# Attention over 16 heads of width 8: from masked 106-row matmuls to one 32-row group per head

## The chip, the cores and the metric

The kernel runs on one NeuronCore of a Trainium2 chip. The metric is the device time of one launch in microseconds (us), the median of three runs. The program was also run once under the hardware profiler; all rows shown here come from that one execution.

## The reference

Four blocks follow one another on x of shape (4, 1024, 128), float32: attention with an ALiBi bias, a mixture of nine experts, a linear attention with decay, and the experts again. Only the first is touched by the change:

```python
q, k, v = proj(Wq, bq), proj(Wk, bk), proj(Wv, bv)        # (4, 1024, 16 heads, 8) from layernorm(x)
scores = jnp.einsum('bqhd,bkhd->bhqk', q, k) / sqrt(8)
scores = scores + bias[None, :, None, :]                  # -(slope of the head * key position)
attn = jax.nn.softmax(scores, axis=-1)
out = jnp.einsum('bhqk,bkhd->bqhd', attn, v).reshape(B, L, D)
x = x + out @ Wo.T + bo
```

## The kernel before

`build_program` calls `attention_phase`, then `expert_phase`, `decay_phase` and `expert_phase`. Everything below is in `attention_phase` (L160 to L710).

The work is cut into 16 units: four sequences b times four groups g of four heads. Within a unit the softmax needs the largest score of each query ahead of the exponentials, so every score is computed twice. `score_unit` (L317, matmul L325) makes scores with queries on partitions, 128 queries by 512 keys, and VectorE takes their maximum (`take_max`, L571): 64 such tiles for a unit, eight query tiles by four heads by two halves of the keys. `tscore` (L329, matmul L335) makes them again transposed, 128 keys by 512 queries, with the negated maximum as two more rows of the contraction, and ScalarE takes the exponential (`exponential`, L499). `values` (L349, matmul L361) multiplies the exponentials of four heads with the padded values `Vp`, float32, each head into its own 32 partitions of bankO.

Precision is kept by splitting queries and keys in a high and a low part (float32r), stacked three times 32 rows: high-high, low-high, high-low. All four heads of the group share these 96 rows of Q. K exists once per head, with the other heads' rows zeroed by a mask (L690, on GpSimd). Rows 96 and 97 carry the bias, rows 98 to 105 the maxima of four heads in two parts. So every score matmul contracts over 98 or 106 rows.

A unit is 16 blocks, k = 0 to 15: two halves of the queries (qh) by eight key tiles (kt). Each engine has its order written out. In a block TensorE issues

```python
tscore(k, 0) score(0) tscore(k, 1) score(1) values(k - 1) tscore(k, 2) score(2) tscore(k, 3) score(3) [extra]
```

where the scores are those of a later unit (three blocks ahead, `AHEAD`), and the extra is one item of `MISC` (L230): a projection for the unit after next (`project`, L305), the transposes of the result (`transpose_u`, L369, and `transpose_on`, L377), the output projection (L384), or `aux` (L313), which brings the maxima from `M2` back through TensorE into rows of Q. All extras share one bank, bankM. bankT and bankS are rings of three banks each; `values(k - 1)` waits until the four exponentials of block k - 1 are done (L359). ScalarE copies the sums out of bankO after each half (`take_u`, L504), and the first `values` of the next half waits for it. Most units run in a hardware loop over b.

Ahead of the blocks stand the layer norm, as a phase with a barrier at its end, and the 64 score tiles of unit 0, which VectorE's maxima pace. In the last unit no scores of a later unit are left, so TensorE issues only tscore and values.

Of the kernel before, what the change touches and what calls it, by code (L numbers as in the profile page):

```python
# [9 lines left out]
ds = bass.ds  # L10
# [149 lines left out]
def attention_phase(nc, X, XT, ident, ident_in, c, w, load, scratch):  # L160
# [7 lines left out]

    AUX = 3 * GE
    NROW_S = AUX + 2
    NROW_T = NROW_S + 2 * HG
    ROTATE = 3

    def last_user(u, units):


        return u - ROTATE if u >= ROTATE else max(v for v in range(units) if v % ROTATE == u) - units

    with ExitStack() as ctx:
# [3 lines left out]
        Wq3 = sb("Wq3", [D, G, AUX]); Wk3 = sb("Wk3", [D, G, AUX])  # L185
        bq3 = sb("bq3", [AUX, G]); bk3 = sb("bk3", [AUX, G]); bq3s = sb("bq3s", [AUX, G])
        WvT = sb("WvT", [D, D]); WoT = sb("WoT", [D, D])
        bvb = sb("bvb", [P, D]); bob = sb("bob", [P, D])
        masks = sb("masks", [AUX, HG])
        V = sb("V", [P, TILES, D])  # L190
        Vp = sb("Vp", [P, TB, H, VW])
        Q = [sb(f"Q{g}", [P, L], F32R) for g in range(G)]
        K = [sb(f"K{g}", [P, HG, L], F32R) for g in range(G)]
        Tq = sb("Tq", [AUX, L]); Tk = sb("Tk", [AUX, L]); Kc = sb("Kc", [AUX, L])
        E = sb("E", [P, 2, HG, BANK])
        hmax = sb("hmax", [P, 2, TB * HG, QH])
        nmax = sb("nmax", [P, TB, HG])
        M2 = sb("M2", [P, TB, VW])
        U = sb("U", [P, L])
        rden = sb("rden", [P, TH * HG])  # L200
        On = sb("On", [P, TB, D])
        ones = U
        OnT = sb("OnT", [P, L])

        (w_loaded, const_loaded, bias_set, zero_done, x_biased) = sem(
            "w_loaded", "const_loaded", "bias_set", "zero_done", "x_biased")
        (proj_ready, proj_taken, q_high, k_high, k_low, k_copies, q_done, k_done) = sem(
            "proj_ready", "proj_taken", "q_high", "k_high", "k_low", "k_copies", "q_done", "k_done")
        (score_ready, max_taken, max_joined, max_high, aux_in, aux_ready, aux_taken) = sem(
            "score_ready", "max_taken", "max_joined", "max_high", "aux_in", "aux_ready", "aux_taken")  # L210
        (tscore_ready, exp_done, pv_done, u_taken) = sem("tscore_ready", "exp_done", "pv_done", "u_taken")
        (ut_ready, rden_done, on_done, ont_ready, ont_taken, y_ready, y_added) = sem(
            "ut_ready", "rden_done", "on_done", "ont_ready", "ont_taken", "y_ready", "y_added")
        (v_ready, v_taken, vp_done) = sem("v_ready", "v_taken", "vp_done")

        S_UNITS = TB * HG * QH
        T_UNITS = QH * TB * HG
        BLOCKS = QH * TB
        PER_BLOCK = S_UNITS // BLOCKS
        AHEAD = 3  # L220

        def score_units(k, now, later):


            m = PER_BLOCK * (k + AHEAD)
            ahead, m = 1 + m // S_UNITS, m % S_UNITS
            return [(ahead, m + i) for i in range(PER_BLOCK)] if (now, later)[ahead - 1] else []


        MISC = {1: ("K", 0), 2: ("K", 1), 3: ("Q", 0), 4: ("Q", 1), 5: ("T", 0), 6: ("T", 1),  # L230
                8: ("G", 0), 9: ("G", 1), 11: ("Y", 0), 12: ("Y", 1), 14: ("A", 0), 15: ("A", 1)}

        def misc(k, s, project, score, after):

            kind, h = MISC.get(k, (None, 0))
            ok = {"K": project, "Q": project, "A": score, "T": after, "G": after and s == 0,
                  "Y": after and s == 0}.get(kind, False)
            return (kind, h) if ok else None

        weights = ((Wq3[:], w["Wq3"]), (Wk3[:], w["Wk3"]), (bq3[:], w["bq3"]), (bk3[:], w["bk3"]),  # L240
                   (WvT[:], w["WvT"]), (WoT[:], w["WoT"]), (masks[:], c["masks"]),
                   (bvb[:], w["bv"].partition_broadcast(P)), (bob[:], w["bo"].partition_broadcast(P)))

        zeros = sb("zeros", [P, BANK])
        zeros_set, cleared = sem("zeros_set", "cleared")

        def load_all(sp, loaded):
            load(sp, loaded)
            for dst, src in weights:
                sp.dma_start(dst, src).then_inc(w_loaded, 16)  # L250

            sp.wait_ge(zeros_set, 1)
            for place in scratch.values():
                sp.dma_start(place.rearrange("(p n m) d -> p n (m d)", p=P, m=BANK // D),
                             zeros[:].unsqueeze(1).broadcast_to([P, SLOT_TILES * D // BANK, BANK]))\
                    .then_inc(cleared, 16)
            sp.wait_ge(w_loaded, 16 * len(weights))

        def constants(block):
            @block.gpsimd  # L260
            def _(pool):
                for g in range(G):
                    pool.dma_start(K[g][AUX:NROW_T, :, :].rearrange("p h k -> p (h k)"), c["key_aux"][g])\
                        .then_inc(const_loaded, 16)
                count = [0]

                def alone(ins):

                    count[0] += 1
                    ins.then_inc(zero_done, 1)  # L270
                    pool.wait_ge(zero_done, count[0])
# [21 lines left out]
        with nc.Block() as block:  # L293
            @block.sync
            def _(sp):
                sp.wait_ge(cleared, 16 * len(scratch))
# [1490 lines left out]
```

## Time and profile before

| | |
|---|---|
| median of three runs | 1989.09 us (1988.19 to 1992.72) |
| span of the profiled execution | 2086.8 us |
| TensorE, VectorE, ScalarE, GpSimd busy | 1651.1, 1093.8, 902.5, 571.8 us |
| first tscore of unit 0 | 100.2 us from the start |
| last values of unit 15 | 1016.8 us from the start |

The profiled execution's own time is its span, 2086.8 us, the time from its first to its last instruction; no other time of it is given. It is 4.9% above the median of the unprofiled runs. Times in the rows are counted from the start of that span. A matmul record ends later than the next can start, since matmuls are pipelined: the distance between starts tells the pace.

### The profile page before, as it was taken

The numbers are of one execution on the slowest core, as the hardware profiler recorded it, in microseconds if no ns is written. First come the engines' busy times: TensorE is split into PE (matmuls) and PEld (weight loads), VectorE is DVE, ScalarE is ACT, GpSimd is POOL, SyncE is SP. The second block draws the span as 40 slices with busy tenths as digits, with TensorE's granted clock in tenths as the row PEclk, the third lists the DMA queues.
The fourth block names the chain that finished last, engine by engine and source line by source line (L and its number), as shares of the span: only waits on it lengthen the run. The fifth ranks groups of instructions, "written<-read, shape, count | busy, mean of one in ns | idle before, by whom it ended". The sixth has DMA issues, their size and how long they took to land. (4 is left out here: it accounts for less than half of the span.)

```text
span 2086.8 us, 32437 instructions
## 1 busy us (share of the span) xinstructions
PE 1651.1 (79%) x8928; PEld 953.1 (46%) x8929; DVE 1093.8 (52%) x2392; ACT 902.5 (43%) x1760; POOL 571.8 (27%) x548
## 2 busy tenths in 40 slices
PE   4899999999999999999632698902899972289890
PEld 2544544545454544554331576701444442167670
DVE  5877777777777777774232122224455553222222
ACT  2266666666666666667510243404222210034340
POOL 3422222112222222110054105453212205410635
PEclk7899999999999999999856899955999985589995
DMA  9000000000000000000121112110000001111222
GB/s 268 1 1 1 1 1 1 3 1 1 1 1 2 1 1 1 1 1 1 42 90 54 45 55 70 56 50 11 1 1 0 0 3 39 55 49 50 74 72 66
DMA packets 69399, 61.23 MB, mean 29 GB/s; under 512 B 8296, under 2 KB 59624, under 8 KB 68840
## 3 DMA queue, kind: packets, MB, share of 16 engines
q1 hardware_dynamic: 39824, 31.66, 4.9%
q0 software_dynamic: 8320, 17.45, 3.0%
q10 hardware_dynamic: 21120, 10.49, 1.8%
q8 instruction: 64, 1.05, 0.2%
q14 instruction: 71, 0.58, 0.1%
HBM read 28.12 MB, written 31.46 MB: 29 GB/s over the span
## 5 line engine op out<-in xcount | busy, mean ns | idle before, releaser
L571 DVE TENSOR_REDUCE attn_hmax<-attn_bankS 128x1 f32<-128x512 f32 x1024 | 644.9, 684 | 206.9 <-PE attn_bankS L325 203.3
L499 ACT ACTIVATE attn_E<-attn_bankT 128x512 f32<-128x512 f32 x1024 | 546.7, 598 | 272.1 <-PE attn_bankT L335 266.3
L335 PE MATMUL attn_bankT<-attn_Q,attn_K 106*128 106x512 f32 x1024 | 458.5, 454 | 5.3 <-ACT attn_E L499 3.1
L325 PE MATMUL attn_bankS<-attn_K,attn_Q 98*128 98x512 f32 x1024 | 418.8, 415 | 22.6 <-DVE attn_hmax L571 17.7
L335 PEld LDWEIGHTS attn_bankT<-attn_Q,attn_K 106*128 106x128 f32 x1024 | 192.3, 189 | 274.5 <-ACT attn_E L499 237.8
L1208 DVE TENSOR_TENSOR ffn_hidden<-ffn_bank,ffn_gated 128x352 f32<-128x352 f32 x160 | 83.9, 525 | 371.8 <-ACT ffn_gated L1167 296.6
L361 PE MATMUL attn_bankO<-attn_E,attn_Vp 128*32 128x512 f32 x2048 | 272.7, 604 | 6.5 <-ACT attn_U L504 5.4
L325 PEld LDWEIGHTS attn_bankS<-attn_K,attn_Q 98*128 98x128 f32 x1024 | 197.2, 193 | 96.8 <-DVE attn_hmax L571 50.5
L1101 PE MATMUL ffn_bank<-w,ffn_xT 128*128 x640 | 226.3, 478 | 7.2 <-issue 4.2
L684 POOL TENSOR_TENSOR attn_Kc<-attn_Tk,attn_Kc 32x1024 f32<-32x1024 f32 x15 | 35.6, 2373 | 667.9 <-DVE attn_Kc L563 667.9
L1016 POOL DMA_INDIRECT tokens<-ffn_XN,ffn_slots x128 | 124.0, 969 | 309.5 <-DVE ffn_slots L885 234.5
L1253 POOL DMA_INDIRECT ffn_pair<-results,ffn_slots x128 | 122.5, 957 | 311.7 <-DMA results<-ffn_y 211.3
L1167 ACT ACTIVATE ffn_gated<-ffn_bank 128x352 f32<-128x352 f32 x160 | 74.1, 463 | 240.6 <-PE ffn_bank L1101 176.2
L1592 DVE TENSOR_TENSOR decay_Am<-decay_bankA,decay_Dm 128x512 f32<-128x512 f32 x128 | 88.4, 690 | 117.5 <-PE decay_bankA L1446 117.3
L1123 PE MATMUL ffn_bankY<-w,ffn_hT 128*128 x960 | 140.7, 284 | 10.0 <-issue 9.9
L1446 PE MATMUL decay_bankA<-decay_qm,decay_km 128*128 128x512 f32 x256 | 140.6, 637 | 6.2 <-ACT decay_km L1543 6.2
L1101 PEld LDWEIGHTS ffn_bank<-w,ffn_xT 128*128 128x128 f32 x640 | 113.9, 198 | 47.9 <-issue 15.8
L1123 PEld LDWEIGHTS ffn_bankY<-w,ffn_hT 128*128 128x128 f32 x960 | 123.8, 197 | 18.2 <-issue 18.2
L1112 PE MATMUL ffn_bankH<-ident,ffn_hidden 128*128 128x128 f32 x480 | 82.2, 282 | 58.7 <-issue 51.7
L690 POOL TENSOR_TENSOR attn_K<-attn_Kc,attn_masks 96x1024 fp32r<-96x1024 f32 x60 | 118.0, 1995 | 2.3 <-POOL attn_Kc L684 2.1
L1112 PEld LDWEIGHTS ffn_bankH<-ident,ffn_hidden 128*128 128x128 f32 x480 | 62.2, 145 | 108.0 <-issue 84.2
L1173 ACT COPY ffn_hT<-ffn_bankH 128x384 f32<-128x384 f32 x160 | 76.0, 475 | 37.1 <-remote 21.3
(182 smaller groups left out, 1380.7 us busy)
## 6 DMA issues: line engine op xcount, KB each, us to landing
ffn_x<-tokens SPq DMA_DIRECT2D x40, 256.0 KB
results<-ffn_y ACTq DMA_DIRECT2D x40, 256.0 KB
tokens<-attn_zeros SPq DMA_DIRECT2D x1, 5120.0 KB, 16.8
results<-attn_zeros SPq DMA_DIRECT2D x1, 5120.0 KB, 28.8
X<-in_x SPq DMA_DIRECT2D x4, 512.0 KB, 16.0
tokens<-ffn_XN,ffn_slots POOLq DMA_INDIRECT x128
ffn_pair<-results,ffn_slots POOLq DMA_INDIRECT x128
out_dram<-X SPq DMA_DIRECT2D x4, 512.0 KB
```

The source lines that it names most:

```text
L325: nc.tensor.matmul(bankS[m % ROTATE][:], Q[g][0:NROW_S, qt * P:(qt + 1) * P], K[g][0:NROW_S, j, kh * BANK:(kh + 1) * BANK], start=True, st ...
L335: nc.tensor.matmul(bankT[u % ROTATE][:], K[g][0:NROW_T, j, kt * P:(kt + 1) * P], Q[g][0:NROW_T, qh * BANK:(qh + 1) * BANK], start=True, st ...
L361: last = nc.tensor.matmul(bankO[32 * j:32 * j + VW, :], Vp[:, kt, g * HG + j, :], E[:, k % 2, j, :], start=(kt == 0), stop=(kt == TB - 1))
L499: nc.scalar.activation(E[:, k % 2, j, :], bankT[(HG * k + j) % ROTATE][:], ACT.Exp)\
L571: nc.vector.reduce_max(hmax[:, g % 2, m // QH, m % QH:m % QH + 1], bankS[m % ROTATE][:], AX.X)\
L690: last = nc.gpsimd.tensor_tensor(K[g][0:AUX, j, :], Kc[:], masks[:, j:j + 1].broadcast_to([AUX, L]), ALU.mult)
L1016: pool.indirect_dma_start(tokens[:, :], bass.IndirectOffsetOnAxis(slots[:, t, k:k + 1], 0), XN[:, t, :], None).then_inc(scattered[h], 16)
L1101: last = nc.tensor.matmul(bank[:, 0:HID], xT[:, p, (k % TH) * P:(k % TH + 1) * P], W13[:, ds(e, 1), :], start=True, stop=True)
L1112: last = nc.tensor.transpose(bankH[:, t * P:(t + 1) * P], hidden[:, k % 2, t * P:(t + 1) * P], ident[:])
L1123: last = nc.tensor.matmul(bankY[k // TH][:, (k % TH) * P:(k % TH + 1) * P], hT[:, k % 2, t * P:(t + 1) * P], w2e[:, t * D:(t + 1) * D], st ...
L1253: pool.indirect_dma_start(pair[:, t % RING, k, :], None, results[:, :], bass.IndirectOffsetOnAxis(slots[:, t, k:k + 1], 0))\
L1446: nc.tensor.matmul(bankA[u % 2][:], km[:, p, j, b * P:(b + 1) * P], qm[:, p, :, b * P:(b + 1) * P], start=True, stop=True).then_inc(a_read ...
```

## The change

`attention_phase` is rewritten; the other phases stay.

- **Row groups.** Head j has rows 32j to 32j + 27 of Q and K: three times 8 rows for the parts, two for the bias, two for its maximum. K is no longer copied per head, and a score matmul contracts over 26 or 28 rows at partition 32j. The bias enters K through a small second matmul in the key projection. The split is four operations of 128x1024 on GpSimd per unit.
- **Maxima.** Two matmuls fill a pair of banks with 128 queries by 1024 keys; one reduce of 128x1024 takes the negated maximum. There are 512 such pairs. bankS is a ring of two pairs, and the transposes of the result and the output projection (`U`, `Y`) take slots in it.
- **T ring.** bankT has three banks, which also serve projections (`P`), transposes of the normalised output (`N`) and the prelude. bankM is gone.
- **Spreading the maxima.** After the 16 pairs of a half (4 query tiles by 4 heads), VectorE splits them in two parts, transposes in 32x32 squares (`turn_maxima`), and SyncE moves them into rows 26 and 27 of each group of Q by eight DMAs. The first exponent of the half waits for all eight.
- **Lead.** Maxima run 22 pairs (`LEAD`, eleven blocks) ahead of the exponents; the turn of half h comes after pair 16h + 19, two blocks ahead of the half's first block 8h.
- **Prelude and form.** The layer norm's work stands inside the same block, with no barrier behind it; all loops are unrolled. Padding of the values moves from VectorE to GpSimd, with two buffers.

```diff
+                def maximum(i, kh):
+                    h, m = divmod(i, ITEMS)
+                    n, qh = divmod(h, QH)
+                    qt, j = qh * TH + m // HG, m % HG
...
+                    rows = slice(32 * j, 32 * j + NROW_S)
+                    mm = nc.tensor.matmul(bank[:, kh * BANK:(kh + 1) * BANK], Q[n % G][rows, qt * P:(qt + 1) * P],
+                                          K[n % G][rows, kh * BANK:(kh + 1) * BANK], start=True, stop=True)
+                def exponent(kb, j, opens):
+                    h, kt = divmod(kb, KT)
+                    n, qh = divmod(h, QH)
+                    if opens and kt == 0:
+                        pe.wait_ge(max_in[h % 2], 16 * 8 * (h // 2 + 1))
+                    bank = slot(("E", kb, j))
+                    rows = slice(32 * j, 32 * j + NROW_T)
...
+        def t_extra(kb):
+
+            n, k = divmod(kb, QH * KT)
+            if k in (6, 8, 10, 12) and n + 2 < UNITS:
+                return ("P", n + 2, (k - 6) // 2)
+            if n % G == 0 and n and k in (7, 9):
+                return ("N", n // G - 1, (k - 7) // 2)
+            return None
+
+        def s_extra(kb):
+
+            n, k = divmod(kb, QH * KT)
+            if k == 3 and n:
+                return ("U", n - 1)
+            if n % G == 0 and n and k == 12:
+                return ("Y", n // G - 1)
+            return None
+
+        def order(kb):
+            return (0, 3, 1, 2) if kb % 2 == 0 else (2, 1, 3, 0)
...
+                for kb in range(BLOCKS):
+                    i = 2 * kb + LEAD
+                    js = order(kb)
+                    exponent(kb, js[0], True)
+                    if i < MAXIMA:
+                        maximum(i, 0)
+                    exponent(kb, js[1], False)
+                    if i < MAXIMA:
+                        maximum(i, 1)
+                    if kb:
+                        values(kb - 1)
+                    exponent(kb, js[2], False)
+                    if i < MAXIMA:
+                        maximum(i + 1, 0)
+                    exponent(kb, js[3], False)
+                    if i < MAXIMA:
+                        maximum(i + 1, 1)
...
+                def spread_maxima(h):
+                    n, qh = divmod(h, QH)
+                    sp.wait_ge(max_turned, h + 1)
+                    for e in range(MAX_ROWS):
+                        rows = Q[n % G][MAX0 + e:P:32, qh * BANK:(qh + 1) * BANK].bitcast(F32)
+                        rows = rows.rearrange("j (t a r) -> j a t r", t=TH, a=4)
+                        for a in range(4):
+                            sp.dma_start(rows[:, a], MT[32 * a + HG * e:32 * a + HG * (e + 1), :, :])\
+                                .then_inc(max_in[h % 2], 16)
...
+                    nc.vector.tensor_reduce(nmax[:, h % 2, m // HG, m % HG:m % HG + 1], bank[:], AX.X, ALU.max,
+                                            negate=True).then_inc(s_taken, 1)
...
+                        if ITEMS <= i < MAXIMA + ITEMS and i % ITEMS == 3:
+                            turn_maxima(i // ITEMS - 1)
```

## Rows read from the trace of the kernel before

**Rows 1.** The page: span, TensorE's busy time, granted clock in 40 slices.
```profile
span 2086.8 us, 32437 instructions
PE 1651.1 (79%) x8928; PEld 953.1 (46%) x8929; DVE 1093.8 (52%) x2392; ACT 902.5 (43%) x1760; POOL 571.8 (27%) x548
...
PEclk7899999999999999999856899955999985589995
```

**Rows 2.** Busy time by stretch: length, busy (count) by engine, clock, DMA share.
```profile
400.00:700.00 300.00, 290.97 (x1491) 150.09 (x1489) 225.97 (x375) 197.67 (x371) 63.22 (x30) 1.00 0.01 1
```

**Rows 3.** Groups: line, engine, out<-in, count | busy us, mean ns | idle before, releaser.
```profile
L335 PE MATMUL attn_bankT<-attn_Q,attn_K 106*128 106x512 f32 x1024 | 458.5, 454 | 5.3 <-ACT attn_E L499 3.1 <-ACT attn_Q L492 2.2
...
L361 PE MATMUL attn_bankO<-attn_E,attn_Vp 128*32 128x512 f32 x2048 | 272.7, 604 | 6.5 <-ACT attn_U L504 5.4 <-ACT attn_E L499 0.9
L571 DVE TENSOR_REDUCE attn_hmax<-attn_bankS 128x1 f32<-128x512 f32 x1024 | 644.9, 684 | 206.9 <-PE attn_bankS L325 203.3 <-DVE attn_On L594 2.8
...
L594 DVE TENSOR_TENSOR attn_On<-attn_bankM,attn_rden 128x128 f32<-128x128 f32 x32 | 9.3, 292 | 1.1
L499 ACT ACTIVATE attn_E<-attn_bankT 128x512 f32<-128x512 f32 x1024 | 546.7, 598 | 272.1 <-PE attn_bankT L335 266.3 <-issue 5.0
L695 POOL TENSOR_TENSOR attn_Q<-attn_Tq,attn_Q 32x1024 fp32r<-32x1024 f32 x15 | 35.6, 2374 | 2.8 <-POOL attn_K L690 2.0 <-DVE attn_Q L567 0.7
```

**Rows 4.** Timeline of TensorE, middle of unit 6: start us, us, instruction, count.
```profile
502.06 0.40 PE L335 MATMUL attn_bankT<-attn_Q,attn_K 106*128 106x512 f32 x1
502.29 0.39 PE L325 MATMUL attn_bankS<-attn_K,attn_Q 98*128 98x512 f32 x1
502.61 1.06 PE L361 MATMUL attn_bankO<-attn_E,attn_Vp 128*32 128x512 f32 x8
503.61 0.50 PE L335 MATMUL attn_bankT<-attn_Q,attn_K 106*128 106x512 f32 x1
```

**Rows 5.** Timeline of TensorE, then ScalarE, in the last unit.
```profile
998.09 1.07 PE L361 MATMUL attn_bankO<-attn_E,attn_Vp 128*32 128x512 f32 x8 [0.48 <-ACT attn_U L504]
...
1003.43 1.06 PE L361 MATMUL attn_bankO<-attn_E,attn_Vp 128*32 128x512 f32 x8
1004.43 0.96 PE L335 MATMUL attn_bankT<-attn_Q,attn_K 106*128 106x512 f32 x3
1005.62 0.50 PE L335 MATMUL attn_bankT<-attn_Q,attn_K 106*128 106x512 f32 x1 [0.23 <-ACT attn_E L499]
1006.10 1.07 PE L361 MATMUL attn_bankO<-attn_E,attn_Vp 128*32 128x512 f32 x8
...
1004.97 2.07 ACT L499 ACTIVATE attn_E<-attn_bankT 128x512 f32<-128x512 f32 x4 [0.60 <-PE attn_bankT L335]
```

**Rows 6.** SyncE's queue, two issues; a DMA's size and time to landing.
```profile
18.90 0.43 SPq L250 DMA_DIRECT2D attn_masks<-const_masks  x1
19.37 0.43 SPq L250 DMA_DIRECT2D attn_bvb<-weight_bv  x1
...
decay_WqT<-weight_b_WqT SPq DMA_DIRECT2D x1, 64.0 KB, 1.8
```

**Rows 7.** Timeline of TensorE: extras in the blocks.
```profile
516.54 1.02 PE L305 MATMUL attn_bankM<-XT,attn_Wk 128*96 x2
...
988.47 0.60 PE L369 MATMUL attn_bankM<-ident,attn_U 128*128 128x128 f32 x4
```

**Rows 8.** Timeline of TensorE: the same operation before and after idling.
```profile
89.73 1.03 PE L313 MATMUL attn_bankM<-ident,attn_M 128*32 128x128 f32 x8 [1.57 <-DVE attn_M L584]
91.44 1.92 PE L313 MATMUL attn_bankM<-ident,attn_M 128*32 128x128 f32 x8 [0.68 <-ACT attn_Q L492]
```

**Rows 9.** Timelines: VectorE's first maxima, TensorE's first tscore and last values.
```profile
45.15 4.87 DVE L571 TENSOR_REDUCE attn_hmax<-attn_bankS 128x1 f32<-128x512 f32 x8 [0.95 <-PE attn_bankS L325]
...
100.24 0.63 PE L335 MATMUL attn_bankT<-attn_Q,attn_K 106*128 106x512 f32 x1
...
1016.80 1.06 PE L361 MATMUL attn_bankO<-attn_E,attn_Vp 128*32 128x512 f32 x8 [0.94 <-ACT attn_E L499]
```

More of the change, by code:

```diff
@@ L214, in attention_phase @@
[L214 to L231, printed above, removed]
@@ new lines, in pair, with turn_tokens @@
+                def pair(item):
+                    i = s_at[item]
+                    if i >= S_PAIRS:
+                        pe.wait_ge(s_taken, i - S_PAIRS + 1)
+                    return bankS[i % S_PAIRS]
+                def turn_tokens(q):
+                    pe.wait_ge(normed, q + 1)
+                    bank = slot(("X", q))
+                    for t in range(TH):
+                        last = nc.tensor.transpose(bank[:, t * P:(t + 1) * P],
+                                                   xn[:, q % XN_SLOTS, t * P:(t + 1) * P], ident[:])
+                    last.then_inc(t_ready, 1)
@@ L473, in _, with turn_values @@
-                for h in range(2):
-                    pe.wait_ge(*free_at[0])
-                    out_project(B - 1, h)
-                    free_at[0] = (y_added, 2 * (B - 1) + h + 1)
+                def turn_values(n):
+                    pe.wait_ge(u_taken, QH * (n + 1))
+                    bank = pair(("U", n))
+                    for t in range(Q_TILES):
+                        last = nc.tensor.transpose(bank[:, t * P:(t + 1) * P], U[:, t * P:(t + 1) * P], ident[:])
+                    last.then_inc(s_ready, 1)
@@ new lines, in turn_outputs, with out_project @@
+                def turn_outputs(b, h):
+                    pe.wait_ge(s_taken, s_at["U", G * (b + 1) - 1] + 1)
+                    bank = slot(("N", b, h))
+                    for t in range(TH):
+                        last = nc.tensor.transpose(bank[:, t * P:(t + 1) * P], On[:, h * TH + t, :], ident[:])
+                    last.then_inc(t_ready, 1)
+                def out_project(b):
+                    pe.wait_ge(t_taken, t_at["N", b, 1] + 1)
+                    bank = pair(("Y", b))
+                    for t in range(Q_TILES):
+                        last = nc.tensor.matmul(bank[:, t * D:(t + 1) * D], OnT[:, t * P:(t + 1) * P], WoT[:],
+                                                start=True, stop=True)
+                    last.then_inc(s_ready, 1)
@@ new lines, in _ @@
+                for kb in range(BLOCKS):
+                    for j in order(kb):
+                        exponent(kb, j)
+                    if kb and kb % KT == 0:
+                        take_sums(kb // KT - 1)
+                    extra = t_extra(kb)
+                    if extra and extra[0] == "P":
+                        take_projection(extra[1], extra[2])
+                    elif extra:
+                        take_outputs(extra[1], extra[2])
+                take_sums(HALVES_A - 1)
```

787 lines of the change are left out of this document (362 added, 425 removed).

## The prediction, made before the changed kernel ran

> **What bounds the kernel now.** I read the page first: TensorE is busy 79% of a span of 2086.8 us, and its clock is full through the attention [rows 1]. The table of stretches then says who sets the pace there: from 400 to 700 us TensorE is busy 291 of 300 us, VectorE 226, ScalarE 198 [rows 2]. The groups say with what: 1024 transposed and 1024 direct score matmuls and the value matmuls; VectorE's and ScalarE's idle time ends at TensorE's scores, while TensorE hardly waits for anybody [rows 3]. The timeline gives prices. Two neighbouring score matmuls start 0.23 us apart, whether they contract over 98 or 106 rows; the four value products occupy 1.00 us from start to the next score, and the matmul ahead of them costs 0.32 instead of 0.23 [rows 4]. A plain block is then 8 x 0.235 + 1.19 = 3.07 us of TensorE, and with the extras 256 blocks fill the stretch from 100.24 to 1016.80 us, 916.6 us [rows 9].
>
> The last unit shows what stands behind TensorE. There the four direct scores of a block are gone, and still a block takes 1006.10 - 1003.43 = 2.67 us, although TensorE needs only 4 x 0.235 + 1.19 = 2.13 [rows 5]. It is a loop through two engines: values start; 1.00 us later the third exponent matmul of the block; 0.54 us after that ScalarE begins; two exponentials, 0.49 + 0.60 us (four take 2.07), end at 2.63; then the next values may start, 0.04 later. The order of issue makes this loop, since exponents 2 and 3 of block k stand behind values(k - 1) and ahead of values(k). The new order keeps it.
>
> **The change, part by part.** *Row groups.* The arithmetic per matmul falls, but a matmul's 512 columns cost what they did. The gain can only come from neighbours in different row groups running at once. No matmul of that kind is in the trace; the nearest rows are the value products, whose four column groups together take 1.00 us for eight records of 0.60 [rows 3, 4]. The order 0,2,3,2 | values | 1,3,2,3 lets two or three overlap. Bounds for the eight: serial 1.88 us, two at a time 0.94. TensorE has 2.67 - 1.19 = 1.48 us for them before it binds, 0.185 us each. I take the lower end, as the column groups do the like, and so a block of 2.67 us, set by the loop: 256 x 2.67 = 683.5 us. The Trainium skill (TensorE: Matmul & The Clock Gate, Part 3) states a measured 3.07 times for four row tiles of 512 columns, by which the eight would take 0.61 us; no run here shows it yet, and the block would be 2.67 all the same.
>
> *Two banks at once.* VectorE spaces 128x512 reduces by (4.87 - 0.68)/7 = 0.60 us [rows 9]. One over 1024 columns lies between 0.60 and 1.20; I take 1.20, as the columns dominate: 2.40 us a block, under the loop, hence worth nothing in the blocks. The ring of two pairs holds: a pair refilled behind values has 2.67 us to be read.
>
> *Sums.* Each half keeps its wait for the copy out of bankO, 0.48 us [rows 5]: 32 x 0.48 = 15.4.
>
> *Maxima spread by DMA.* What leaves is 32 calls of aux, 1.03 us of TensorE each [rows 8], which are part of the 916.6. What comes is a chain with a wait at its end, and everything later in TensorE's queue (direct scores, values) stands behind that wait, and with it VectorE and ScalarE. Count from the start of the values in block 8h - 2. The last matmul of pair 16h + 19 starts at 1.00 + 0.10 + 0.21 = 1.31, its record ends at 1.71, the reduce runs 1.81 to 3.01, the 32x32 transpose (a 128x128 operation of VectorE took 0.29 [rows 3]) ends at 3.30. SyncE issues eight DMAs, 0.47 us apart whatever their size: 3.3. The last lands after 1.8, if as fast as the quickest load [rows 6]: 8.4, and the first exponent of block 8h can start at 8.5, its values at 9.0. Without the wait they would start at 2 x 2.67 = 5.3. So each half but the first stalls 3.7 us: 31 x 3.7 = 114.7. Bounds: issue 0.43 apart and landing at 1.3 gives 2.9; landing at 2.8 gives 4.7. The Trainium skill (DMA: Bandwidth & Descriptors, Anatomy of one DMA) gives about 2.0 us of fixed cost per DMA; with it the stalls would be 6 us more in all.
>
> *Clock.* TensorE idles about 4.3 us in each stall. After an idle time of only 1.57 us the same eight records went from 1.03 to 1.92 us [rows 8], full to half clock. A block at half clock costs 0.85 more for values and about 0.35 more for the exponent ahead of ScalarE, 1.2; part of the low stretch lies in the stall itself, so I take 0.8 a half, 24.8 in all. Bounds: nothing, and four blocks of 1.2.
>
> *Extras.* A projection (1.02 us [rows 7]) now takes a slot of the T ring: the second exponent of the next block waits for the exponential two places on, and values move from 2.67 to about 3.2. Of four in a unit the one at k = 6 falls into the stall: 14 x 3 x 0.6 = 25.2. U takes a pair: the next pair waits for VectorE until 3.1, values start at 3.6: 15 x 0.95 = 14.3. Y and N: 3 x 3.1 = 9.3. GpSimd's four operations at up to 2.4 us [rows 3] are 9.5 us per unit of 54, two units ahead: hidden; uncovered they would cost that once.
>
> Sum: 683.5 + 15.4 + 114.7 + 24.8 + 25.2 + 14.3 + 9.3 = 887.2, against 916.6: 29.4 less.
>
> *Prelude.* Eleven weight loads issue at 0.47 from about 16 us and are in at about 25; four projections at half clock end near 34; 18 more items of at most 1.02 us [rows 7] end near 52.5; 20 reduces of 1.20 and three small operations reach 77.3, the eight DMAs 82.6, against 100.24 [rows 9]: 17.6 less. The end (one copy, two transposes, one addition instead of a chain through one bank) saves some 1.5. Unrolled code costs nothing visible, as unit 0 was unrolled before too.
>
> In all 48.5 us less: 2087 to 2038 us for the profiled execution. That execution is 98 us above the median, and I can't say where; none of my terms rests on a rare delay, so I subtract the same from the median: 1989 - 49 = **1940 us**.
>
> **Rivals.** *(a) The groups don't overlap.* Then TensorE binds at 3.07 us and pays its extras on top, while the stall stays (the turn comes later with the slower block, 3.7): 16 x (49.1 + 7.4 + 6.0) = 1000, less 25 for the last two units that lack projections and scores, 975; with the clock 25: 83 more than 916.6, prelude and end 19 less: about 2053 us. For it: each matmul loads its own 128 columns of weights, and no row group runs beside another in this trace. Against: column groups do. It decides from about 0.22 us a matmul upwards; a block of 2.92 instead of 2.67 eats the 49 us.
>
> *(b) The maxima are in time.* If issue and landing took under 1.6 us together there is no stall and no fall of the clock: 887 - 115 - 25 = 747, about 1989 - 170 - 19 = 1800 us. Against: eight issues alone take 3.3 us. Between this and the forecast lies a half stall, 1870.
>
> *(c) The clock stays low after stalls*, three to four blocks each time: 31 x 4.2 = 130 instead of 25: about 2045 us. For it: the fall after 1.57 us. Against: through the attention it stayed full [rows 1], in the last unit too, where TensorE needs 2.13 of 2.67 us.
>
> *(d) The change does as its numbers suggest* and VectorE's 2.4 us set the block. Then 256 blocks are 69 us shorter, but the stall grows by 0.54 each: 1888 us. The Trainium skill (TensorEngine Tiling (Array Packing), PSUM Bottleneck) says that the copy out of PSUM may become the bound once tiles run side by side; the loop of the last unit, 2.67, speaks against it.
>
> **How the numbers follow.** Chances: forecast 0.56, (a) 0.15, (b) and the half stall 0.13, (c) 0.10, (d) 0.06. The forecast's own range is 1890 to 1990: stalls of 2.9 to 4.7 are -25 to +31, a block 0.1 longer 19, clock and prelude 20. The range for 8 in 10 is 1850 to 2035: it leaves out the full (b) and the upper parts of (a) and (c). A measurement of this kernel tells 0.2%, 4 us, from no change. Faster: 0.51 of the forecast's 0.56, (b), (d) and a small part of (c): 0.72. Within 0.2%: 0.04. Slower: (a), most of (c): 0.24.
>
> **What would show it.** Two score matmuls of different groups starting some ns apart, and eight in under 1.48 us; values 2.67 us apart in a plain block; VectorE busy about 85% between stalls; 32 times a wait of TensorE's for the DMAs into Q, ending about 5.2 us after the transpose; half clock for a few us behind it; first exponent near 83 us. The forecast is wrong if the issue of a DMA of 16 runs of 128 bytes is much cheaper than 0.47 us, if the groups run one by one, or if the clock doesn't come back.

## The result: 2332 us, a ratio of 1.172

The changed kernel takes 2332.45 us (median of four runs, 2327.18 to 2335.98) against 1989.26: 1.172 times the kernel before, 95% interval 1.1692 to 1.1748. The forecast was 1940, at most 2035. Sign and size are both wrong.

The page of the changed kernel; the groups give busy us and mean ns, then the idle time before them:

```profile
span 2328.9 us, 28004 instructions
PE 1902.9 (82%) x8704; PEld 828.2 (36%) x8705; DVE 1026.3 (44%) x1850; ACT 891.5 (38%) x1728; POOL 497.2 (21%) x519
...
PEclk9555555555555555555555555999758999669995
...
L585 DVE TENSOR_REDUCE attn_nmax<-attn_bankS 128x1 f32<-128x1024 f32 x512 | 618.0, 1223 | 615.4 <-PE attn_bankS L365 615.4
L504 ACT ACTIVATE attn_E<-attn_bankT 128x512 f32<-128x512 f32 x1024 | 550.0, 597 | 615.2 <-PE attn_bankT L377 613.9
L377 PE MATMUL attn_bankT<-attn_Q,attn_K 28*128 28x512 f32 x1024 | 464.9, 756 | 108.9 <-DMA attn_Q<-attn_MT 62.9
L365 PE MATMUL attn_bankS<-attn_K,attn_Q 26*128 26x512 f32 x1024 | 549.6, 713 | 4.1 <-DVE attn_nmax L585 3.6
...
L681 POOL TENSOR_SCALAR attn_highk<-attn_Tk,attn_lowk 128x1024 fp32r<-128x1024 f32 x16 | 17.9, 1121 | 662.7 <-ACT attn_Tk L492 605.1
```

Its table of stretches, with columns as in [rows 2], for the same 300 us:

```profile
400.00:700.00 300.00, 278.60 (x1042) 84.77 (x1042) 148.80 (x148) 140.83 (x261) 30.11 (x17) 0.51 0.00 1
```

The clock row has a 5 where [rows 1] has a 9: for nearly all the time from 52 to 1370 us TensorE was granted half clock, 1.2 instead of 2.4 GHz. In the stretch the clock is 0.51 instead of 1.00, and TensorE is busy 279 of 300 us with 1042 instead of 1491 records. VectorE and ScalarE wait for it, over 600 us each. A matmul record of 713 to 756 ns is the same instruction that takes about 490 at full clock, as TensorE's timeline around one of the few rises shows (L338 is a projection, L413 the output projection, L391 the values):

```profile
465.14 2.08 PE L338 MATMUL attn_bankT<-XT,attn_Wq 128*128 128x512 f32 x2
467.01 2.71 PE L413 MATMUL attn_bankS<-attn_WoT,attn_OnT 128*128 128x128 f32 x16
469.65 0.50 PE L377 MATMUL attn_bankT<-attn_Q,attn_K 28*128 28x512 f32 x1
469.65 0.49 PE L365 MATMUL attn_bankS<-attn_K,attn_Q 26*128 26x512 f32 x1
469.65 0.50 PE L377 MATMUL attn_bankT<-attn_Q,attn_K 28*128 28x512 f32 x1
469.99 0.39 PE L365 MATMUL attn_bankS<-attn_K,attn_Q 26*128 26x512 f32 x1
470.31 1.07 PE L391 MATMUL attn_bankO<-attn_E,attn_Vp 128*32 128x512 f32 x8
471.30 0.49 PE L377 MATMUL attn_bankT<-attn_Q,attn_K 28*128 28x512 f32 x1
...
472.54 0.50 PE L377 MATMUL attn_bankT<-attn_Q,attn_K 28*128 28x512 f32 x1
...
473.03 1.06 PE L391 MATMUL attn_bankO<-attn_E,attn_Vp 128*32 128x512 f32 x8
...
475.27 0.67 PE L377 MATMUL attn_bankT<-attn_Q,attn_K 28*128 28x512 f32 x1 [0.21 <-ACT attn_E L504]
475.87 1.94 PE L391 MATMUL attn_bankO<-attn_E,attn_Vp 128*32 128x512 f32 x8
...
481.89 0.79 PE L377 MATMUL attn_bankT<-attn_Q,attn_K 28*128 28x512 f32 x1 [2.94 <-DMA attn_Q<-attn_MT]
```

Three things are to be seen. Matmuls of different row groups start together, three at 469.65, and the four with the switch to values take 0.66 us. A plain block at full clock is 473.03 - 470.31 = 2.72 us. And the clock falls at 475.27, when the score records go from 0.50 to 0.67 and the values from 1.06 to 1.94, six us after it rose and **before** TensorE waits for the DMA at 481.89. It rose right behind a projection and among sixteen matmuls of the output projection, all over 128 rows; there are three such rises, at 470, 795 and 1121 us. The other two ended with a wait of 4.4 us for the DMAs, about 10 us after the rise.

The clock had been lost long before the first such wait. In the prelude, where each pair of maxima waits for VectorE, it falls at 52 us; the first exponent waits for its DMAs at 79 (TensorE's timeline):

```profile
50.70 0.73 PE L365 MATMUL attn_bankS<-attn_K,attn_Q 26*128 26x512 f32 x2 [0.40 <-DVE attn_nmax L585]
51.84 0.95 PE L365 MATMUL attn_bankS<-attn_K,attn_Q 26*128 26x512 f32 x2 [0.41 <-DVE attn_nmax L585]
52.97 2.35 PE L365 MATMUL attn_bankS<-attn_K,attn_Q 26*128 26x512 f32 x4 [0.18 <-DVE attn_nmax L585]
```

From there it stayed at half until the output projection at 468 us. The kernel before also lost it in its prelude, at 91 us [rows 8], but its own score matmuls over 98 and 106 rows, one behind another, brought it back 14 us later:

```profile
104.08 0.63 PE L325 MATMUL attn_bankS<-attn_K,attn_Q 98*128 98x512 f32 x1
...
104.83 0.40 PE L325 MATMUL attn_bankS<-attn_K,attn_Q 98*128 98x512 f32 x1
```

A block at half clock on TensorE's timeline, then ScalarE's four exponentials of a block at full and at half clock:

```profile
582.83 1.94 PE L391 MATMUL attn_bankO<-attn_E,attn_Vp 128*32 128x512 f32 x8
584.69 0.79 PE L377 MATMUL attn_bankT<-attn_Q,attn_K 28*128 28x512 f32 x1
...
586.23 0.79 PE L377 MATMUL attn_bankT<-attn_Q,attn_K 28*128 28x512 f32 x1 [0.31 <-ACT attn_E L504]
...
586.96 1.94 PE L391 MATMUL attn_bankO<-attn_E,attn_Vp 128*32 128x512 f32 x8
```
```profile
471.89 2.07 ACT L504 ACTIVATE attn_E<-attn_bankT 128x512 f32<-128x512 f32 x4 [0.56 <-PE attn_bankT L377]
...
585.58 2.13 ACT L504 ACTIVATE attn_E<-attn_bankT 128x512 f32<-128x512 f32 x4 [1.93 <-PE attn_bankT L377]
```

The block takes 586.96 - 582.83 = 4.13 us. The loop: values start; after 1.86 us the exponent; after 0.89 ScalarE begins; after 0.65 (one exponential and the hand-over) the block's fourth exponent matmul, which waited 0.31 us for that T bank; 0.73 later the next values. At full clock the same steps are 0.99, 0.59, 0.65 and 0.49, in sum 2.72.

The stall at a half's start, on SyncE's queue and TensorE:

```profile
595.67 4.53 SPq L302 DMA_DIRECT2D attn_Q<-attn_MT  x8
```
```profile
601.30 0.79 PE L377 MATMUL attn_bankT<-attn_Q,attn_K 28*128 28x512 f32 x1 [0.54 <-DMA attn_Q<-attn_MT]
```

First exponent and last values of the attention, against 100.24 and 1016.80 in [rows 9]:

```profile
79.32 0.79 PE L377 MATMUL attn_bankT<-attn_Q,attn_K 28*128 28x512 f32 x1 [4.87 <-DMA attn_Q<-attn_MT]
...
1358.14 1.93 PE L391 MATMUL attn_bankO<-attn_E,attn_Vp 128*32 128x512 f32 x8 [1.23 <-ACT attn_E L504]
```

The attention ends 341 us later, which is the 343 of the medians. Counting the 255 distances between the values of neighbouring blocks, and calling a block full when its first value record took under 0.8 us: 8 full, of median 2.73, and 247 half, of median 4.13. I use this count ("full blocks") for every kernel below.

One caution for reading the ratios. The kernel before ran at 1989 us in some sets of runs (the results, e5 to e8 and e13 to e16) and at 2089 to 2093 in others (e1 to e4 and e9 to e12), so each ratio is to the kernel before in the same set. Ratios and their intervals are of the runs within 1.5% of a kernel's quickest, and medians are of all its runs. Where two sets are compared I use the time of the last values, which does not move (1016.8 and 1019.0 us in the kernel before at 2086.8 and 1988.3). Full blocks and last values are those of the profiled execution, which in e1, e7, e8 and e13 was the slowest of the runs or within 1 us of it.

### The profile page after: what moved, and what is told of

It reads as the page before. It is cut to its first block and busy times, and to the rows that moved or that the text cites. A ratio compares the mean times of both kernels' runs of the same rounds, so it can differ in the third digit from the quotient of the medians.

```text
span 2328.9 us, 28004 instructions
## 1 busy us (share of the span) xinstructions
PE 1902.9 (82%) x8704; PEld 828.2 (36%) x8705; DVE 1026.3 (44%) x1850; ACT 891.5 (38%) x1728; POOL 497.2 (21%) x519
## 5 line engine op out<-in xcount | busy, mean ns | idle before, releaser
L585 DVE TENSOR_REDUCE attn_nmax<-attn_bankS 128x1 f32<-128x1024 f32 x512 | 618.0, 1223 | 615.4 <-PE attn_bankS L365 615.4
L377 PE MATMUL attn_bankT<-attn_Q,attn_K 28*128 28x512 f32 x1024 | 464.9, 756 | 108.9 <-DMA attn_Q<-attn_MT 62.9
L365 PE MATMUL attn_bankS<-attn_K,attn_Q 26*128 26x512 f32 x1024 | 549.6, 713 | 4.1 <-DVE attn_nmax L585 3.6
L391 PE MATMUL attn_bankO<-attn_E,attn_Vp 128*32 128x512 f32 x2048 | 488.5, 1047 | 5.1 <-ACT attn_U L511 3.5
L377 PEld LDWEIGHTS attn_bankT<-attn_Q,attn_K 28*128 28x128 f32 x1024 | 176.8, 286 | 697.4 <-issue 379.9
L365 PEld LDWEIGHTS attn_bankS<-attn_K,attn_Q 26*128 26x128 f32 x1024 | 225.0, 295 | 22.2 <-DVE attn_nmax L585 19.3
L1098 PE MATMUL ffn_bank<-w,ffn_xT 128*128 x640 | 221.6, 470 | 6.0 <-ACT ffn_xT L1158 3.2
L681 POOL TENSOR_SCALAR attn_highk<-attn_Tk,attn_lowk 128x1024 fp32r<-128x1024 f32 x16 | 17.9, 1121 | 662.7 <-ACT attn_Tk L492 605.1
L391 PEld LDWEIGHTS attn_bankO<-attn_E,attn_Vp 128*32 128x32 f32 x2048 | 51.6, 139 | 138.8 <-ACT attn_E L504 59.3
```

The lines of the kernel that those rows point to most:

```text
L365: mm = nc.tensor.matmul(bank[:, kh * BANK:(kh + 1) * BANK], Q[n % G][rows, qt * P:(qt + 1) * P], K[n % G][rows, kh * BANK:(kh + 1) * BANK] ...
L377: nc.tensor.matmul(bank[:], K[n % G][rows, kt * P:(kt + 1) * P], Q[n % G][rows, qh * BANK:(qh + 1) * BANK], start=True, stop=True)\
L391: last = nc.tensor.matmul(bankO[32 * j:32 * j + VW, :], Vp[:, b % 2, kt, g * HG + j, :], E[:, kb % E_BLOCKS, j, :], start=(kt == 0), stop= ...
L585: nc.vector.tensor_reduce(nmax[:, h % 2, m // HG, m % HG:m % HG + 1], bank[:], AX.X, ALU.max, negate=True).then_inc(s_taken, 1)
L1098: last = nc.tensor.matmul(bank[:, 0:HID], xT[:, p, (k % TH) * P:(k % TH + 1) * P], W13[:, ds(e, 1), :], start=True, stop=True)
```

## The experiments

All leave the computation as it is; added matmuls write a bank that the next exponent overwrites. The theories have the letters of the expectations: **A**, the stream of matmuls over 26 and 28 of 128 rows doesn't hold the clock up, stall or no stall; **B**, the idle time of the stall for the DMAs brings it down and keeps it there; **C**, what counts is how much of the time some matmul runs, whatever its rows.

**e5 and e6: both kernels again, unchanged.**

> The changed kernel again, beside the kernel before on the chip of this call, since the runs of the kernel before lie at 1989 us in one call and at 2089 us in another. If only the kernel before differs between chips, this stays at about 2332 us and the ratio is 1.116; if both differ alike, it is near 2440 us and the ratio 1.17.

> The kernel before, unchanged, with a profile of its own, as a measure of what differs between two executions of one program: ratio 1.00. Its clock stays full from the first blocks to the last values, and the attention blocks fill 916 us as in the first profile; if the chips differ, it is in the stages behind them.

Measured: 2331.0 us, 1.1715 [1.1697, 1.1732], 8 full blocks; and 1989.64 us, 1.0001 [0.9982, 1.002]. The low clock repeats on another occasion.

**e1 and e7: the maxima earlier.** `AHEAD` counts blocks; the lead is 16 + 2 x `AHEAD` pairs. Six and five in place of three move the turn of the maxima from two blocks ahead of their use to five and four. The second line is a wait of VectorE's for its own earlier work.

```diff
-    AHEAD = 3
+    AHEAD = 6        (e7: 5)
...
+                    if n:
+                        dve.wait_ge(s_taken, s_at["U", n - 1] + 1)
```

> The lead of the maxima grows from three blocks to six, so that the DMAs into Q have landed before the half begins. Theory A (the clock falls because a score matmul fills 26 or 28 of 128 rows of the array): the waits for the DMAs vanish (2 to 3 us in each of 31 halves at half clock), the granted clock stays at 0.5 through the blocks, a plain block stays at 4.13 us, and the time is 2240 to 2280 us. Theory B (the idle time of the stall brings the clock down and keeps it there): with the stall gone the clock is full, a block is 2.7 us and the time below 1850 us.

> A lead of five blocks instead of three. The lead of six had a side effect: it moved the maxima's row groups onto those of the exponents beside them, so the overlap was partly lost; with five the groups stay apart and the DMAs still have time (two blocks more, 5.4 us at full clock, against the stall of 3.7 us). Theory A: half clock for most of the time, plain blocks of 4.13 us there, full clock for some tens of us behind each output projection; 2230 to 2270 us, within 1.5% of the lead of six. Theory B (idle time alone): mostly full clock, below 1900 us.

Measured: e1 2259.28 us, 1.0776 [1.072, 1.0832], 93 full blocks, last values at 1205.5. e7 2215.64 us over four runs from 2120.14 to 2263.72, without an interval, near 1.11; 15 full blocks in its profile (the slowest of the four), last values at 1290.6. No wait for a DMA stands in either; the stall is gone, and still most blocks are at half clock, so B alone is not it. Theory A had e7 about right (2230 to 2270 us). That e1 lies in its range (2240 to 2280) is luck: in that set the kernel before was 100 us slower than at the time of the forecast, and by the ratio the forecast was 1.13 to 1.15. TensorE's timeline of e1 at one fall:

```profile
586.38 1.06 PE L391 MATMUL attn_bankO<-attn_E,attn_Vp 128*32 128x512 f32 x8
...
588.62 0.50 PE L377 MATMUL attn_bankT<-attn_Q,attn_K 28*128 28x512 f32 x1
...
589.64 1.93 PE L391 MATMUL attn_bankO<-attn_E,attn_Vp 128*32 128x512 f32 x8 [0.53 <-ACT attn_U L511]
```

Here 0.53 us of idling, the wait for the copy out of bankO, was followed by half clock until 745 us; the kernel before has the like of it, 0.48 us in [rows 5], and stays full. In e1 itself nine such waits met full clock, and a fall stood right behind two of them and within a block of a third. Six also puts the maxima into the same row groups as the neighbouring exponents, so the later kernels use five.

**e2, e3, e4: more matmuls in each block.** Two at the start of every block, behind the wait for the maxima; over 128 rows in e2 and e4, over 28 in e3. e4 adds `AHEAD = 6`.

```diff
+                    if opens:
+                        for _ in range(2):
+                            nc.tensor.matmul(bank[:], K[n % G][:, kt * P:(kt + 1) * P],     (e3: [rows, ...])
+                                             Q[n % G][:, qh * BANK:(qh + 1) * BANK], start=True, stop=True)
```

> Two matmuls over all 128 rows (128x128 weights, 512 columns) are added at the start of each block; their result is overwritten by the first exponent matmul of the block, so the output doesn't change. The stall stays. Theory A: the array is filled enough, the clock is full, the two matmuls fit into the slack of the 2.67 us loop, and the time falls to 1900 to 1990 us although TensorE does more. Theory B: the stall is as before, the clock stays at half, and two more matmuls at 0.43 us make every block about 0.9 us longer: some 2550 us.

> The control of the run with two filling matmuls: the same two matmuls per block, but over the 28 rows of the head that follows. Theory A: as many matmuls and columns, but few rows, so the clock stays at half and each block is 0.85 to 0.9 us longer: 2500 to 2560 us. Theory C (what counts is how much of the time some matmul streams, whatever its rows): the clock rises as in the run with full rows, and the time is near 1950 us.

> Both: two matmuls over 128 rows in each block and a lead of six blocks. Both theories give full clock and no stall; theory A gives the block of 2.7 to 2.8 us set by the loop values, exponent matmul, two exponentials, values: 1810 to 1860 us, faster than both kernels. If the clock is full but the block is not 2.7 us, the loop was misread.

Measured: e2 2577.7 us, 1.2288 [1.2216, 1.236], 65 full blocks; e3 2466.11 us, 1.1802 [1.1784, 1.182], 9; e4 2372.85 us (2371.78, 2373.92, 2376.53 and once 2168.59), 170. Theory A's numbers for e2 and e4 missed by over 400 us, because I had taken the clock to be up all the time once filled; for e2, B's 2550 was nearer. In e3 neither C's 1950 nor A's 2500 to 2560 came: the narrow pair costs a block nothing (4.13 us at half clock, as without it), since it runs beside its neighbours. The wide rows do raise the clock (65 and 170 full blocks against 9), and with the stall in place it comes down again, in e2 13 of 14 times after 14 to 23 us. A block at half clock with the two costs 5.31 us, 1.18 more than 4.13, so filling pays only where the clock then stays.

**e8 and e9: lead, fill, and fill in the prelude; wide against narrow.** `AHEAD = 5` with its wait; two matmuls at the start of each block, ahead of the wait for the maxima, four more in block 6 of each unit, and three behind each pair of the lead.

```diff
+                def wide(bank, n, count):
+                    for _ in range(count):
+                        nc.tensor.matmul(bank[:], K[n % G][:, 0:P], K[n % G][:, 0:BANK], start=True, stop=True)
...
+                    if opens:
+                        wide(bank, n, 2 + (4 if kb % 16 == 6 else 0))
...
+                    wide(slot(("E", 0, order(0)[0])), 0, 3)      (in the loop over the lead)
```

In e9 the rows are `32 * j:32 * j + 28`.

> A lead of five blocks; two matmuls over 128 rows ahead of every block (operands from K alone, result overwritten), four more ahead of one block of each unit, and three behind each of the 26 leading pairs, so that the clock is up when the blocks begin. Theory A: the clock stays up nearly throughout; a plain block costs 1.0 (values) + 3 x 0.66 us = 2.98 us and the whole is 50 to 80 us below the kernel before. If the clock falls again and again, the share of half clock decides: 2250 us at one half of the time. Theory B gives full clock as well, so this run measures what full clock is worth, not which theory holds.

> The run with two wide matmuls per block and the wide lead, lead of five blocks, with one change: each added matmul runs over the 28 rows of one head instead of 128. Same places, same number, same columns. Theory A (rows filled decide the clock): half clock through nearly all blocks, ratio to the kernel before 1.10 to 1.18. Theory C (time streamed decides, rows don't matter): full clock as in the wide version, ratio 0.95 to 0.98.

Measured: **e8 1955.4 us** (1934.49 to 1967.95), 0.9746 [0.9718, 0.9773], or 0.983 by the medians, 244 full blocks, last values at 995.2, ahead of the kernel before. A block at full clock has the forecast 2.98 us. e9 2128.4 us, 1.0175 [1.0153, 1.0198], 165 full blocks, last values 1057.3. The clock row and the 300 us of e8:

```profile
PEclk8999997599999999999965899965899995599995
```
```profile
400.00:700.00 300.00, 297.04 (x1695) 112.41 (x1694) 219.53 (x218) 206.37 (x378) 37.23 (x21) 0.99 0.01 2
```

VectorE is busy 220 us where the changed kernel has 149: with the clock back the same code goes half as fast again. Both kernels do the same work with the same count of columns; only rows differ. In the prelude the narrow ones lose the clock (e9, then e8, TensorE's timeline; a lone L365 goes from 0.50 to 0.79 us):

```profile
56.73 0.50 PE L365 MATMUL attn_bankS<-attn_K,attn_Q 26*128 26x512 f32 x1
...
57.86 0.79 PE L365 MATMUL attn_bankS<-attn_K,attn_Q 26*128 26x512 f32 x1
```
```profile
57.73 0.73 PE L365 MATMUL attn_bankS<-attn_K,attn_Q 26*128 26x512 f32 x2
58.39 0.97 PE L372 MATMUL attn_bankT<-attn_K 128*128 128x512 f32 x3
```

Both forecasts for e9 missed (A 1.10 to 1.18, C 0.95 to 0.98), and the full blocks say why. What the narrow fill lacks is mostly the rise: e9 ran at half clock from the prelude to the first output projection, 76 blocks, and had 165 full blocks of the 179 behind it, where e8 had 178 and e7, with the same lead and no fill, 15. So two narrow matmuls a block go far towards **holding** a clock that is up. The first fall of e9 behind that projection (645 us), and both falls of e8 (320 and 573 us), came behind an idle time of TensorE that the trace gives no releaser for, 2.5 us in e9 and 1.7 in e8:

```profile
572.35 0.46 PE L365 MATMUL attn_bankS<-attn_K,attn_Q 26*128 26x512 f32 x1 [1.69 <-issue]
```

**e10 and e11: less fill**, otherwise e8: one in each block (`1 + (4 if ...)`), and none (`0 + (4 if ...)`).

> One wide matmul per block instead of two (the burst of one block per unit and the lead stay). At full clock the block is back at the 2.73 us of the loop, 0.25 us less than with two, 64 us in all: ratio 0.94 to 0.95 if one is enough to hold the clock. If it isn't, the clock falls at the half boundaries as in the runs with a longer lead alone: ratio 1.00 to 1.10. Theory A says that holding gets less certain with fewer wide rows; theory B (idle time) sees one wide matmul per block as no difference and predicts the first.

> No wide matmul per block; only the wide lead, and four before one block in each unit. The blocks begin at full clock and there is no stall. Theory A: the clock falls within the first one or two units, comes back at a burst now and then, full clock in a fifth to a half of the blocks: ratio 1.03 to 1.12. Theory B: nothing idles, so the clock stays up: ratio 0.93 to 0.95.

Measured: e10 2117.68 us over runs of 2036.86, 2039.96, 2195.41 and 2198.39; the lower two give 0.9744 [0.9719, 0.9769], the upper two 1.05; its profile is of the latter, with 171 full blocks. e11 2238.92 us, 1.0687 [1.0656, 1.0718], 108 full blocks. Less fill holds the clock for a smaller part of the time, and at one a block it goes either way. e11 came out as A forecast it (a fifth to a half of the blocks, 1.03 to 1.12), and not as B did (0.93 to 0.95).

**e12: e8 with `AHEAD` left at 3**, and without VectorE's wait that belongs to the longer lead, so that the stall is back.

```diff
-    AHEAD = 5
+    AHEAD = 3
...
-                    if n:
-                        dve.wait_ge(s_taken, s_at["U", n - 1] + 1)
```

> The wide version with two per block and the wide lead, but with the changed kernel's lead of three blocks, so that the wait for the eight DMAs is back. At full clock it should idle TensorE by 9.1 - 2 x 2.98 = 3.1 us in each of 31 halves, 97 us: ratio 1.02 to 1.03 if the clock holds through it. If the stall brings the clock down as well, plain blocks of 5.3 us follow it: ratio 1.08 to 1.25. This separates what the stall does by itself from what the narrow rows do.

Measured: 2518.2 us, 1.2034 [1.1981, 1.2086], 103 full blocks, last values at 1438.7 against 995.2. Its waits from 90 to 1440 us (total, times, longest):

```profile
PE attn_bankT L383 <- DMA attn_Q<-attn_MT: 66.6, 30, 3.6
```

The stall itself is 67 us of the 443 that it costs. Another 329 are the clock (141 more blocks at half, 5.31 instead of 2.98 us each); the last 48 I did not separate. Of the 30 waits, 24 found the clock full, and with each of the 24 it fell (the values behind the wait are at half); the other six found it at half. It came back 17 to 72 us later. So B is right as far as it goes: given a stream that holds the clock, the stall takes it away. The Trainium skill (TensorE: Matmul & The Clock Gate, Part 1, HAM oscillation) says that a DMA wait in every tile can bring the clock down every time; e12 shows that, with a fall for each wait that found the clock full, while e7 shows the low clock with no such wait.

**e13 and e14: a burst.** `AHEAD = 5`, no fill but twelve matmuls at the start of block 6 of each unit: over 128 rows, and over 28.

```diff
+                    if opens:
+                        wide(bank, n, (12 if kb % 16 == 6 else 0))
```

> Lead of five blocks, nothing added but a burst of twelve matmuls over 128 rows ahead of one block (k = 6) of each unit. Theory A (the rows filled count, for the rise too): each of the 16 bursts, 5.1 us dense at half clock and next to a wide projection, brings the clock up; it falls again some blocks or units later for want of rows. Full clock in 80 or more of 256 blocks, ratio 1.00 to 1.08. If only the output projections raise it, as before, full clock in 10 to 40 blocks, ratio near 1.13.

> The same twelve matmuls in the same places over 28 rows each. Theory A: they raise nothing; full clock only behind the output projections, as with the lead of five alone (15 of 256 blocks in its profile), ratio 1.10 to 1.14. Theory C (time streamed counts, whatever the rows): as many rises as with the wide burst, and the same ratio.

Measured in one set: e13 1970.73 us, **0.9865 [0.9839, 0.9892]**, or 0.991 by the medians, 197 full blocks, last values at 1012.8. e14 2254.86 us, 1.1329 [1.1273, 1.1385], 54 full blocks, last values at 1275.9. TensorE's timeline at a burst, of e13, then of e14:

```profile
573.53 1.94 PE L397 MATMUL attn_bankO<-attn_E,attn_Vp 128*32 128x512 f32 x8
...
576.55 5.49 PE L372 MATMUL attn_bankT<-attn_K 128*128 128x512 f32 x12
...
582.73 1.06 PE L397 MATMUL attn_bankO<-attn_E,attn_Vp 128*32 128x512 f32 x8
```
```profile
425.13 1.94 PE L398 MATMUL attn_bankO<-attn_E,attn_Vp 128*32 128x512 f32 x8
...
427.60 4.46 PE L372 MATMUL attn_bankT<-attn_K 28*128 28x512 f32 x10
...
433.27 1.94 PE L398 MATMUL attn_bankO<-attn_E,attn_Vp 128*32 128x512 f32 x8
```

Twelve wide ones at half clock bring the values from 1.94 to 1.06 us, here and at every other burst that met half clock, 11 of 11; as many narrow ones (two more stand between the next matmuls) leave them at 1.94, in 12 of 12. Two more narrow bursts met full clock and lost it, at 554 and 1235 us, with no idle time of TensorE since the values before. In e14 the clock rises only behind the three output projections, as in the changed kernel, and once, in the last unit, behind eight transposes over 128 rows. The count, the columns and the place are the same, so for the rise the rows decide. This was the sharpest test, and e14 fell where A had put its ratio (1.10 to 1.14), though with 54 full blocks for 15; C had put it beside e13. e13 did better than A's number.

**e15 and e16: e8 refined**, with one and two in each block, five and four more in block 6 of each half, two behind each pair of the lead, and two in the wait for the copy out of bankO:

```diff
-                        if h:
-                            pe.wait_ge(u_taken, h)
...
+                    if kt == 0 and h:
+                        if kb + 1 < BLOCKS:
+                            wide(slot(("E", kb + 1, order(kb + 1)[2])), (kb + 1) // (QH * KT), 2)
+                        pe.wait_ge(u_taken, h)
```

> A candidate for a version faster than both: one wide matmul per block, two wide ones in each wait for the copy out of bankO, where TensorE idled 0.5 us and where the falls of the clock were seen, five more before one block of each half, and two instead of three per leading pair. If the small idle at the half boundary was what tipped the clock, it stays up: ratio 0.93 to 0.95, and little spread. If one per block is too few anyway, it falls in some executions: spread of 5% and a ratio up to 1.02.

> The same with two wide matmuls per block. A plain block costs 2.98 us, so at full clock throughout it is 0.96 to 0.975; it should spread less than the version without the filled waits (1934 to 1968 us there).

Measured: 1981.2 us (1967.91 to 2001.33), 0.9932 [0.99, 0.9964], 233 full blocks; and 1997.76 us (1994.86 to 2009.24), 1.0045 [1.0025, 1.0065], 248. Neither comes out as forecast. In both the clock fell in the prelude, where two in place of three stand behind each pair (first values at 105.3 and 110.9 us instead of 95.4). In e16 a plain block at full clock is e8's 2.98 us, but three blocks of each unit, those with the added matmuls, are longer than e8's by 0.92, 0.65 and 0.39 us, about 31 us over 16 units. e8 remains the best by the median.

## Why the prediction was wrong, step by step

**The step that failed** is *Clock*, "0.8 a half, 24.8 in all", with its upper bound of "four blocks of 1.2", and the reason given against rival (c), "through the attention it stayed full". It treated the clock as something that idling takes away for a moment and work gives back. That the clock was full before was a property of the old stream, matmuls over 98 and 106 rows one behind another [rows 4], even where it used 2.13 of 2.67 us [rows 5]; the change took just that stream away. Where the old stream lost the clock, at 91 us, it had it back after 14 us, about the four blocks of the upper bound; in the new one it doesn't come back by itself, and it is lost at 52 us already, without any stall. Rival (c) had the right engine and sign, but with the ceiling of a few blocks after each stall it gave 2045 us and 0.10. The prediction's last sign of being wrong, "if the clock doesn't come back", is the one that came.

**The sum.** From first exponent to last values the forecast was 887.2 us, and the trace has 1358.1 - 79.3 = 1278.8, 391.6 more. Blocks at half clock give 247 x (4.13 - 2.67) = 361 of it. The rest of the stretch, beyond plain blocks, is 1278.8 - 247 x 4.13 - 8 x 2.73 = 237, where stalls, clock, extras and copies were put at 204: 33 more, and I did not separate it further.

- *Price of half clock*: 1.2 us a block forecast, 4.13 - 2.73 = 1.40 measured. The forecast counted the values (0.85; 1.86 - 0.99 = 0.87 measured) and the exponent (0.35; 0.30), and left out the last step (0.73 - 0.49 = 0.24). The size was near; how often was not, 247 times.
- *Overlap* was right: three row groups started within 10 ns of each other, and rival (a) is out. Three side by side took 0.34 us (469.65 to 469.99), where three in sequence are 0.70.
- *Block of 2.67* was near: 2.73 at full clock in every kernel without a fill in its blocks. The loop that closes last goes through the fourth exponent's T bank and not through a second exponential; the two differ by 0.05 us. Rival (d) is out, a reduce of 1024 columns takes 1.22 us (forecast 1.20), and TensorE's waits for VectorE's maxima come to about 4 us, all but 0.4 of it in the prelude.
- *Stall*: 31 x 3.7 forecast; 58 us in 27 waits behind the first. The longer blocks hide a part. The chain was right in kind: eight issues take 4.53 us, 0.57 each (forecast 0.47), and from the first to the use are 601.30 - 595.67 = 5.6 (forecast 5.2 from the transpose on). At e12's higher clock 67 us in 30. Rival (b) is out. The 2.0 us that the prediction takes from the Trainium skill (DMA: Bandwidth & Descriptors, Anatomy of one DMA) stand there for DMAs that GpSimd issues, and these are SyncE's; from the start of the eighth issue to the use are 1.6 us here.
- *GpSimd hidden*: right, 1.12 us an operation where at most 2.4 was allowed.
- *Prelude*: first exponent at 79.3 (forecast 82.6; 100.2 before).

**What the runs establish.** Two causes keep the clock down, and either suffices. The stream is one: without a stall the clock is still low in most blocks (e7, e14), and no stretch of the narrow stream raised it; wide matmuls do (11 of 11 bursts in e13), narrow ones of the same number don't (12 of 12 in e14). The stall is the other: with each of the 24 waits that found the clock full in e12 it was lost. The changed kernel has both.

**What stays open.** Which quantity of the stream holds the clock once it is up: rows alone don't tell it, since e9's narrow fill kept it for 165 of 179 blocks, and narrow matmuls also run beside others and so fill less time. What idle time alone is worth in the narrow stream, since waits of the same 0.53 us were followed by a fall or by nothing. Why TensorE idles without a releaser in e8 and e9. Why e10's runs, e7's and e4's lie so far apart; full blocks are counted in one execution of each.

## What to carry to other kernels

Packing small contractions into row groups takes work off TensorE in time and also in rows, and here the clock went with it: check by the durations of one and the same matmul, in each stage, whether the clock is still full, before crediting the packing with anything. Where it is not, a few full-height matmuls whose result is overwritten can pay for themselves (twelve in a unit of 16 blocks brought e7's 2215.64 us, the median of runs 144 us apart, to e13's 1970.73), provided that no wait on a chain of small DMAs is left; so lengthen the lead first and fill second. A bound taken from how the old stream behaved says nothing about a new one.

## What the runs showed of the hardware that was not expected

- A burst of twelve 128-row matmuls, 5.49 us, brought the clock back each time that it met half clock; one of 28 rows never did.
- An idle time of 0.53 us was followed by half clock for some 150 us (e1), where six more of that length in e1 and thirteen in e9 were not followed by a fall within a block: it does not decide by itself.
- Two narrow matmuls added to each block cost no time (2.73 us at full clock in e9, as without them) and still held the clock for most of the blocks, once an output projection had raised it.
- SyncE's eight small DMAs issue 0.57 us apart, against 0.47 for the loads of [rows 6].
- The kernel before, unchanged, has two levels, 1989 and 2089 us, constant to 0.5% within a set of runs. The 100 us lie behind the attention: from the last values to the end the traces have about 970 or about 1070 us (966 to 973, and 1061 to 1074), whatever the attention, and GpSimd's gathers wait 155 or 211 us for the experts' results. What sets the level was not tried; both were met on the same chip number. It is also the 98 us between the profiled execution and the median that the prediction could not place.
